# Gathers of later blocks spread over more steps: a change to GpSimd's order of work in a DLRM kernel with compressed interactions

## What is computed

```python
def cin_layer(xi, x0, W, b):            # xi [n, Fi, e], x0 [n, 48, e]
    Wr = W.reshape(Fi, 48, -1)
    return relu(jnp.einsum('nie,nje,ijo->noe', xi, x0, Wr) + b[None, :, None])
xs = [x0]                               # x0: the gathered rows, [512, 48, 32]
for W, b in ((W1, b1), (W2, b2), (W3, b3)):
    xs.append(cin_layer(xs[-1], x0, W, b))        # 128 outputs each
z = concatenate(xs, axis=1).sum(axis=-1)
h = concatenate([z, dense_ctx], axis=1)
y = relu(relu(h @ W_top1 + b_top1) @ W_top2 + b_top2) @ W_top3
```

## Time and profile before

| | |
|---|---|
| runs | 2443.72, 2445.55, 2446.77 us; median 2445.55 |
| profiled execution | 2444.75 us; span of its trace 2442.9 |
| TensorE clock granted | 0.984 of full over the span |
| ScalarE's wait for TensorE (L572) | 172.1 us, 403 times |
| GpSimd's wait for ScalarE ahead of L327 | 127.0 us, 128 times |
| GpSimd's wait for a DMA ahead of L350 | 66.5 us, 89 times |
| GpSimd's wait for ScalarE ahead of L373 | 65.8 us, 58 times |
| VectorE's wait for GpSimd ahead of L795 | 54.8 us, 97 times |
| 192 gathers | 202.5 us of GpSimd, 1055 ns each |
| 12 spreads | 13.8 us of GpSimd, 1150 ns each |

### The profile page before, as it was taken

How to read it: one execution, slowest core, us unless ns; L and a number is a source line. 1 busy time by engine, 2 the same in 40 slices (tenths; PEclk the granted TensorE clock), 3 DMA queues, 4 the chain that set the end, 5 groups by cost and what they waited for, 6 DMA issues and landing times.

```text
span 2442.9 us, 68954 instructions
## 1 busy us (share of the span) xinstructions
PE 2325.3 (95%) x14174; PEld 1178.2 (48%) x14174; DVE 2278.7 (93%) x9404; ACT 2117.9 (87%) x7910; POOL 1953.0 (80%) x2134
## 2 busy tenths in 40 slices
PE   1699999999999999999999999999999999999998
PEld 0354454454554554444455445445445555555543
DVE  6499999999999999999999999999999999999995
ACT  4589889889898898888898888988889989999984
POOL 7488888887778888888778888888777777777773
PEclk6799999999999999999999999999999999999999
DMA  5133333333333333333333333333333333333331
GB/s 170 30 68 72 69 66 70 70 69 64 69 70 66 69 72 70 63 72 70 61 70 70 70 64 71 72 65 68 70 62 70 67 69 70 69 70 69 69 64 35
DMA packets 150318, 168.63 MB, mean 69 GB/s; under 512 B 111956, under 2 KB 115671, under 8 KB 150264
## 3 DMA queue, kind: packets, MB, share of 16 engines
q0 software_dynamic: 43008, 137.39, 30.4%
q1 hardware_dynamic: 107256, 30.73, 5.7%
HBM read 12.82 MB, written 0.00 MB: 5 GB/s over the span
## 4 chain that ended last, share of the span: by engine, by line
PE 42%; POOL 16%; issue 13%; ACT 10%; DVE 9%; DMA 8%; DVEq 1%; ACTq 0%; POOLq 0%; SPq 0%
PE y L474 35%; DMA work<-work 8%; ACT work L572 6%; DVE acc L786 5%; PE m L464 5%; POOL part L350 4%; POOL emb L295 3%; POOL part L354 2%; POOL part L352 2%; ACT work L602 1%; POOL psum L357 1%; POOL rest L342 1%; PE m L446 1%; POOL work L327 1%; DVEq L96 1%
## 5 line engine op out<-in xcount | busy, mean ns | idle before, releaser
L474 PE MATMUL y<-whi,xT 128*128 128x512 f16 x6144 | 2006.9, 379 | 38.8 <-DVE acc L786 24.3
L572 ACT ACTIVATE work<-y,xc 128x128 f32<-128x128 f32 x5632 | 1604.9, 417 | 182.7 <-PE y L474 172.1
L786 DVE SCALAR_TENSOR_TENSOR acc<-y,xc,acc 128x128 f32<-128x128 f32 x5632 | 1654.5, 343 | 32.8 <-PE y L474 24.1
L474 PE MATMUL y<-wlo,xT 128*128 128x512 f16 x3072 | 1164.8, 379 | 0.0
L474 PEld LDWEIGHTS y<-whi,xT 128*128 128x128 f16 x6144 | 599.0, 97 | 692.3 <-issue 77.9
L474 PEld LDWEIGHTS y<-wlo,xT 128*128 128x128 f16 x3072 | 300.8, 98 | 227.8 <-issue 0.6
L350 POOL TENSOR_TENSOR part<-work 128x512 f32<-128x512 f32 x256 | 325.4, 1271 | 90.8 <-DMA work<-work 66.5
L362 POOL TENSOR_TENSOR zl<-work,zh 128x1152 f16<-128x1152 f32 x128 | 345.0, 2695 | 8.1 <-ACT work L602 8.1
L327 POOL DMA_DIRECT2D work<-work x256 | 229.2, 895 | 128.4 <-ACT work L572 127.0
L295 POOL DMA_INDIRECT emb<-tbl,ids_sb x192 | 202.5, 1055 | 45.0 <-issue 43.9
L600 ACT ACTIVATE zh<-m 128x512 f16<-128x512 f32 (+1 forms) x384 | 212.2, 553 | 3.1 <-PE m L446 3.1
(11 more groups left out here) (104 smaller groups left out, 2101.3 us busy)
## 6 DMA issues: line engine op xcount, KB each, us to landing
work<-work POOLq DMA_DIRECT2D x256, 512.0 KB, 4.7
xT<-hi SPq DMA_TRANSPOSE x256, 2.7
xT<-lo SPq DMA_TRANSPOSE x256, 2.4
emb<-tbl,ids_sb POOLq DMA_INDIRECT x192, 2.6
xx<-w SPq DMA_DIRECT2D x4, 768.0 KB, 8.7
work<-w SPq DMA_DIRECT2D x4, 768.0 KB, 14.6
x0T<-x0hl SPq DMA_TRANSPOSE x128, 2.2
wt_sb<-W_top SPq DMA_DIRECT2D x1, 768.0 KB, 13.8
```

Of the source, the lines that this page charges most:

```text
L474: ins = nc.tensor.matmul(dst[:], xT[layer][:, parity, a, :], w[layer][:, cols], start=i == 0, stop=i == 2)
L572: nc.scalar.activation(prods[layer][:, a, k * P:(k + 1) * P], bank[:, k * P:(k + 1) * P], ACT.Copy, scale=xc[layer][:, parity, j:j + 1]).t ...
L786: ins = nc.vector.scalar_tensor_tensor(dst, y, col, mine, ALU.mult, ALU.add)
```

## The change

The three later blocks' 144 gathers become one list, handed out by `next_gather`; the twelve spreads become another, of which a step takes the next one if the gathers of its block had all been asked for when the step began. Steps -3 to 0 take two late gathers, steps 1 to 8 an early and a late one, later steps a late one and, if odd, an early one, until the list is empty. The loop over blocks is gone.

```diff
-GATHERS, SPREAD, GROUP = 2, 8, 12
+SPREAD, GROUP, EARLY = 8, 12, 8
...
-            def step(v, parity, b=None, fields=(), columns=None):
+            rows = [(b, f) for b in range(1, NB) for f in range(F)]
+            columns = [(b, e) for b in range(1, NB) for e in range(0, E, SPREAD)]
+            given_out = {"rows": 0, "columns": 0}
+
+            def next_gather():
+                if given_out["rows"] < len(rows):
+                    b, f = rows[given_out["rows"]]
+                    gather(b, (f,))
+                    given_out["rows"] += 1
+
+            def next_spread(asked):
+                i = given_out["columns"]
+                if i < len(columns) and asked >= columns[i][0] * F:
+                    spread(*columns[i], SPREAD)
+                    given_out["columns"] += 1
+
+            def step(v, parity):
                 t0, t2, t3 = v + 3, v + 1, v
+                asked = given_out["rows"]
...
                 if parity == 0 and active(v + 4):
                     x0_scaled(v + 4)
-                gather(b, fields[0:1])
+                if v > 0 and (parity == 1 or v <= EARLY):
+                    next_gather()
                 if parity == 0 and active(v + 4):
                     x0_lo(v + 4)
...
                 if active(t0):
                     squares_lo(t0)
-                gather(b, fields[1:2])
-                if columns:
-                    spread(b, *columns)
+                if v > -4:
+                    next_gather()
+                if -4 < v <= 0:
+                    next_gather()
+                next_spread(asked)
                 if active(t3):
                     sum_rest(1, t3)
 
-            for v in range(-4, 1):
+            for v in range(-4, TILES):
                 step(v, v % 2)
-            for b in range(NB):
-                v = b * E + 1
-                if b + 1 < NB:
-                    for f in range(0, F, GATHERS):
-                        step(v, v % 2, b + 1, fields=range(f, f + GATHERS))
-                        v += 1
-                    for e in range(0, E, SPREAD):
-                        step(v, v % 2, b + 1, columns=(e, SPREAD))
-                        v += 1
-                while v < min((b + 1) * E + 1, TILES):
-                    step(v, v % 2)
-                    v += 1
             sum_all(1, TILES - 1)
```

## The result

The changed kernel takes 2454.16 us (median of 7 runs, 2453.66 to 2455.51) against 2445.55 us (7 runs): ratio 1.0036, 95% interval 1.0025 to 1.0048. It is slower, by 8.6 us, and at the forecast 2454. The span of the profiled execution is 2451.9 us against 2442.9. On this kernel's page GpSimd is as busy as before and VectorE's merge (L807, which was L795) waits longer, 66.7 us for GpSimd against 54.8; that the total came out right doesn't yet say that its terms did.

What follows compares the result with a forecast made beforehand. TensorE was taken to set the pace only without gathers; in gather pairs the late even gather and VectorE's hold add 0.98 us. Terms 0 + 3.9 + 4.4 + 1 = 9.3 on 2444.75 gave 2454 us, range 2445 to 2460.

Steps and rivals of the forecast that it cites:

- The gathers taken away: Early gathers of even steps 10 to 88, hidden under GpSimd's wait for ScalarE's x0hl: removing them saves 32 x 0.
- The late even gather is the cost: Even step's late gather, between layer 3's DMA and the next sums: causes the 0.98 us excess of a gather pair.
- VectorE's hold: L749 and L753 stand while GpSimd runs: 0.29 us of a gather pair's excess; 2.1 in pairs with copies and gathers.
- Four plain pairs: Steps 29 to 32 and 61 to 64 get three gathers a pair: 4 x 0.98 = +3.9 us.
- Four pairs with copies: Steps 25 to 28 and 57 to 60 get three gathers besides their spreads: 4 x 1.1 = +4.4 us.
- The merges' part: In pairs with copies and gathers, the longer stretch from DMA to first sum adds about 1.4 us of merge wait.
- Fill: Two late gathers each in steps -3 to 0 delay the start: +1 us, bounds 0 and 2.5.
- The cover named for steps -3 to -1: GpSimd's waits for ScalarE, 2.71 and 4.16 us, cover the gathers of steps -3 and -1; step -2's lie between such waits.
- A: Rival: GpSimd's load in even steps is the bound, so removing a gather speeds up: 2426 or about 2414 us; chance 0.17.
- B: Rival: new gathers in steps 25 to 32 and 57 to 64 find room: 2447 to 2449 us; chance 0.16.
- C: Rival: copy and gather holds add up, 1 us more a spread pair and fill 2.5: 2460 us; chance 0.08 alone.

Runs made afterwards that it cites:

- early_everywhere: The changed kernel with even steps' early gather kept in all steps, four gathers a pair: 2440.21 us, ratio 0.9988 to the kernel before.
- even_early: The changed kernel with the even step's one gather in its early place from step 9 on: 2428.69 us, ratio 0.9944 to the kernel before.
- under_the_waits: The changed kernel's instructions, every gather and spread placed under an existing wait, none behind squares_lo: 2405.51 us, ratio 0.9837 to the kernel before.

## Why the prediction was right, and where it was not

*The gathers taken away: 0.* Right, by the pairs (436.44 against 436.59), by the wait that grew from 0.57 to 1.79, and by early_everywhere.

*The late even gather is the cost, 0.98 a pair of which 0.29 is VectorE's hold.* Right in the place, not in the shares. even_early takes the gather off, and a pair falls by 0.62 to 35.75: the even late gather is some 0.6. The other 0.35 is the odd step's late gather. under_the_waits moves that gather as well and ends at 35.42. The prediction had it cost only by the hold, but its stretch is 5.47 us long where 4.63 is plain, and in under_the_waits the two held instructions (L766, L770) still take 0.78 a pair, 0.15 less than in even_early, while the pair fell by 0.33. So the stretch is the likelier cause of most of it; no run takes one away without the other. The parts also don't simply add: 0.12 of hold over plain costs nothing there.

*Four plain pairs: +3.9.* Measured +4.3: steps 29 to 32 took 73.3 and steps 61 to 64 72.2, where 72.8 was said.

*Four pairs with copies: +4.4.* Wrong in size, +2.3. They took 38.11, 37.48, 37.90 and 37.48, where 38 or more was said. The step that failed is VectorE's hold, put at 2.1 us a pair (L749 0.4 to 0.5, L753 1.6). It is 1.82, 1.46, 1.71 and 1.48, 1.62 on average, and it lies the other way round: L761 (once L749) has the long one. At 0.48 a pair that is 1.9 us of the 2.1 missing. VectorE's and GpSimd's timelines around an odd step's copy in the changed kernel:

```profile
617.94 0.96 DVE L761 TENSOR_SCALAR mx<-mx 128x2 f32<-128x2 f32 x1
...
619.07 0.51 DVE L765 TENSOR_SCALAR mp<-mx 128x2 uint32<-128x2 uint32 x1
```

```profile
616.94 1.07 POOL L295 DMA_INDIRECT emb<-tbl,ids_sb  x1 [0.17 <-issue]
617.97 0.89 POOL L304 COPY xx<-emb 128x384 f32<-128x384 f32 x1
618.78 0.77 POOL L342 TENSOR_TENSOR rest<-work 128x256 f32<-128x256 f32 x1
```

L761 began while the gather still ran, just ahead of the copy, and came free at 618.90, with the copy's end at 618.86; L765 came free at 619.58, with the rest sum's end at 619.55. I had carried over from the earlier trace rows that one hold spans copy and rest, and had put both on L753. The Trainium skill (SBUF — State Buffer, section "SBUF: two separate sides") has the lock held for one whole instruction. That would fit these two rows if the first hold is counted from the copy's start. The first pair with copies speaks against it, in rows of VectorE and GpSimd:

```profile
580.12 1.31 DVE L761 TENSOR_SCALAR mx<-mx 128x2 f32<-128x2 f32 x1
```

```profile
579.46 1.06 POOL L295 DMA_INDIRECT emb<-tbl,ids_sb  x1 [0.17 <-issue]
580.51 0.88 POOL L304 COPY xx<-emb 128x384 f32<-128x384 f32 x1
```

L761 began 0.66 us into the gather, was not freed at the gather's end at 580.52, and came free at 581.43 with the copy's end at 581.39. So a hold can pass from one GpSimd instruction to the next, here as in the old rows, but it did not go on over the rest sum. Why it stops at one boundary and not at the other, no run shows.

The merges' part was about right: they wait 1.7 us in steps 58 and 59, where 0.13 + 1.4 was expected. And there the two parts, 0.8 + 1.6 = 2.4 over plain, showed as 37.48 - 35.42 = 2.06.

*Fill: +1.* Measured 1.7 at step 25, 1.2 at step 9 (272.14 against 270.91). The cover named for steps -3 to -1 held; step 0's gathers cost, as said.

Against the sum of 9.3 the plain pairs came out 0.4 higher, the fill 0.7, the pairs with copies 2.1 lower, and 0.7 of small differences came on top. They nearly cancel. That the total hit 2454 is in part luck; the mechanism and the sign were not. Of the rivals, A fell by even_early, where the load stayed and the time went. B fell by the steps 29 to 32 and 61 to 64, which found no room, though the four pairs with copies grew by only 0.6 us each instead of 1.1. C's extra didn't come.

## What to carry to other kernels

Before an instruction is moved or thinned out, find the wait behind it on its engine: if the engine waits for another engine's work right after it, and the wait doesn't go to nothing, the instruction is free where it stands, and taking it away only lengthens the wait. A wait for a DMA that the engine itself issues behind the instruction is no such cover. The same instruction between a DMA's issue and the sum that follows may cost much of its length (here 0.6 of 1.2 us, and 0.95 for a second one), so move work to in front of an instruction that waits, by as much as that wait is long (a 1.2 us gather in front of 0.87 us still cost). And spreading work evenly over steps was worth nothing in itself here; it pays where the place is covered and costs in every new step where it is not.

## What the hardware showed that was not expected

- A VectorE instruction on 128x2 elements took 0.15 us alone and up to 1.8 us beside running GpSimd instructions (1.2 beside one tensor sum), and whenever it took over 0.25 us in the kernel before, it ended within 0.05 us of the end of one of them. The same kind of instruction on 128x1 elements (L815) never took over 0.154 us in 256 cases.
- The issue of a gather on GpSimd held it too. VectorE's and GpSimd's timelines of the kernel before, step 3:

```profile
177.89 0.77 DVE L749 TENSOR_SCALAR mx<-mx 128x2 f32<-128x2 f32 x1
```

```profile
177.54 1.07 POOL L295 DMA_INDIRECT emb<-tbl,ids_sb  x1 [0.17 <-issue]
```

L749 came free at 178.66, the gather having ended at 178.61.
